# Experts over gathered tiles of 256 rows, in place of eight experts for every token

## The reference, cut to what matters

```python
x = x + 0.5 * ffn(layernorm(x))          # 8 experts, the best 2 of each token
x = x + attention(layernorm(x))          # 16 heads of 8 channels
x = x + 0.5 * ffn(layernorm(x))          # the same expert weights again

def ffn(x):                              # N = 4096 tokens
    logits = flat @ Wr.T                 # (N, 8)
    weights, ids = top_k(logits, 2)
    weights = softmax(weights)
    h = einsum('nc,efc->nef', flat, W1)  # 512 hidden columns: 256 values, 256 gates
    act = h[..., :256] * silu(h[..., 256:])
    y = einsum('nef,ecf->nec', act, W2)  # 256 -> 128
    return einsum('nec,ne->nc', y, router_weights)   # zero for 6 of the 8 experts
```

## Time and profile before

| | us |
|---|---|
| median of 3 runs (1358.19 to 1359.80) | 1358.84 |
| the profiled execution, whole | 1362.02 |
| its span, first to last instruction | 1360.2 |
| first expert stage and start: to the first product of attention | 356.2 |
| attention, from there to the last copy of its output | 703 |
| second expert stage | 301 |

### The profile page before, as it was taken

The page is one execution under the profiler, slowest core; times in us unless marked ns, Lnnn a source line. Parts: engine busy times, 40 slices in busy tenths (PEclk is TensorE's granted clock), DMA queues, the critical chain, the costliest instruction groups (busy, mean ns, idle before and its releaser), DMA issues.

```text
span 1360.2 us, 32042 instructions
## 1 busy us (share of the span) xinstructions
PE 1269.9 (93%) x10240; PEld 615.2 (45%) x10240; DVE 1112.3 (82%) x2306; ACT 816.2 (60%) x1540; POOL 142.5 (10%) x450
## 2 busy tenths in 40 slices
PE   5999999999899989999998999899989999999998
PEld 3766666666422222222222222222222677767776
DVE  7887877787779888888888888888886677777775
ACT  4433333333158888888888888888888423323332
POOL 1021112210211111111111111111110000000000
PEclk9999999999759999999999999999999999999999
DMA  6010111101221110101001100110011100000000
GB/s 201 1 47 14 36 47 47 47 21 28 67 60 31 31 39 30 29 29 39 30 29 33 36 30 29 37 32 29 29 41 31 40 26 26 26 22 13 24 3 15
DMA packets 52265, 48.49 MB, mean 36 GB/s; under 512 B 10080, under 2 KB 44768, under 8 KB 52192
## 3 DMA queue, kind: packets, MB, share of 16 engines
q1 hardware_dynamic: 52192, 47.61, 12.0%
HBM read 23.86 MB, written 23.33 MB: 35 GB/s over the span
## 4 chain that ended last, share of the span: by engine, by line
PE 82%; ACT 6%; issue 6%; DVE 4%; SPq 1%; ACTq 0%; DMA 0%; DVEq 0%
PE ps L765 22%; PE ps L906 19%; PE ps L893 18%; PE ps L752 15%; ACT probs L661 5%; PE ps L722 2%; PE ps L864 1%; DVE X L1092 1%; PE ps L742 1%; PE ps L686 1%; PE ps L883 1%; PE ps L729 1%; DVE act L1080 1%; PE ps L759 1%; SPq L320 0%
## 5 line engine op out<-in xcount | busy, mean ns | idle before, releaser
L1235 DVE TENSOR_REDUCE mx<-ps 128x1 f32<-128x1024 f32 x512 | 591.9, 1217 | 75.1 <-PE ps L864 69.4
L661 ACT ACTIVATE probs<-ps 128x512 f32<-128x512 f32 x1024 | 568.5, 594 | 93.0 <-PE ps L893 74.0
L906 PE MATMUL ps<-probs,vh 128*32 128x256 f32 x4096 | 329.6, 393 | 56.0 <-ACT probs L661 42.0
L590 ACT ACTIVATE sg<-ps,unscale 128x512 f32<-128x512 f32 x256 | 173.7, 687 | 307.0 <-PE ps L765 285.3
L893 PE MATMUL ps<-Q,K 51*128 51x512 bf16 x1024 | 333.2, 386 | 0.5 <-ACT probs L661 0.2
L864 PE MATMUL ps<-K,Q 48*128 48x512 bf16 x1008 | 328.1, 390 | 2.5 <-DVE mx L1235 2.0
L752 PEld LDWEIGHTS ps<-w,act 128*128 128x128 f32 x2048 | 247.9, 192 | 17.1
L752 PE MATMUL ps<-w,act 128*128 128x128 f32 x2048 | 249.0, 275 | 0.0
L1080 DVE SCALAR_TENSOR_TENSOR act<-ps,unscale,sg 128x512 f32<-128x512 f32 x256 | 183.5, 745 | 58.2 <-PE ps L765 19.8
L765 PE MATMUL ps<-x_hi,w_hi 128*128 128x512 f16 x512 | 194.6, 380 | 10.9 <-DVE act L1080 6.3
L1092 DVE SCALAR_TENSOR_TENSOR X<-ps,rw,X 128x128 f32<-128x128 f32 (+1 forms) x512 | 144.0, 344 | 61.9 <-PE ps L752 61.4
(11 more groups left out here) (84 smaller groups left out, 611.5 us busy)
## 6 DMA issues: line engine op xcount, KB each, us to landing
o_parts<-ot SPq DMA_DIRECT2D x64, 128.0 KB, 1.8
q_stack<-parts SPq DMA_DIRECT2D x48, 128.0 KB, 2.3
k_stack<-parts SPq DMA_DIRECT2D x48, 128.0 KB, 2.3
Q<-q_stack SPq DMA_DIRECT2D x64, 96.0 KB, 2.3
K<-k_stack SPq DMA_DIRECT2D x64, 96.0 KB, 2.3
probs<-w_in SPq DMA_DIRECT2D x8, 256.0 KB, 3.9
att<-o_parts SPq DMA_DIRECT2D x16, 128.0 KB, 2.6
rden<-rdens SPq DMA_DIRECT2D x16, 128.0 KB, 2.5
```

The source lines that it names most:

```text
L590: nc.scalar.activation(sg[:, j, :], hid[2 * j], ACT.Silu, scale=unscale[:, e, 2 + j:3 + j]).then_inc(silu_done, 1)
L661: nc.scalar.activation(probs[:, kb % PSLOTS, j * CH:(j + 1) * CH], score[i], ACT.Exp, scale=SCALE).then_inc(probs_ready, 1)
L906: last = nc.tensor.matmul(opsum[VW * c:VW * (c + 1), :], vh[:, u % 2, kb, :], probs[:, kb % PSLOTS, c * QW:(c + 1) * QW], start=(kb == 0), ...
L1235: nc.vector.tensor_reduce(mx[:, u % 2, t:t + 1], pair.rearrange("p a b -> p (a b)"), AX_X, ALU.max).then_inc(max_read, 1)
```

## The change

An expert stage is made of three steps that follow each other, where before one loop did everything.

1. **Gather** (`gather`, on all engines). For each of 4 batches of 1024 tokens: layernorm scaled by 2^11, router, two best experts. From membership matrices PE computes with small bf16 products (`places`) the place of each token within the region of its expert; a region has room for all tokens. POOL then sends the rows by indirect transfers (`scatter`): 16 for a batch, each 128 rows of 520 bytes (f16 high and low part, the number of the output row, the weight). DVE makes a table of 39 tiles from the counts (`make_table`): expert and first row of each. SP fills the ends of the regions with idle rows (`fill_pads`). 8192 rows need at most 39 tiles of 256, and always 39 are run.
2. **Tiles** (`experts`, written out 39 times). SP loads 256 rows into one of six slots (`load_tile`), PE transposes them, ACT copies them out of PSUM, and the products, silu and multiplication follow with half the former width. The expert comes from the table into a register (`value_load`) on PE, ACT and DVE, the first row into one on SP. DVE multiplies the output by the weight (`weigh`), and POOL sends it by two indirect transfers of 128 rows of 512 bytes to `y_rows` in HBM (`scatter_y`), where a token's two outputs lie side by side. A row slot is free again when the tile's output has landed.
3. **Add** (`add_y`). For each chunk of 512 tokens SP loads the pairs of rows (512 KB), and DVE adds both to X.

After the first stage the layernorm, projections, split and storing for attention now come chunk by chunk behind `add_y`, with no expert between. After attention, the output projection of three batches stands in the last head, that of the fourth in the gather. `store_out` follows `add_y` chunk by chunk. Attention itself is as it was. The diff, cut to its core:

```diff
+TILE = 256
+TH = TILE // P
+PICKS = 2
+TILES = PICKS * N // TILE + E - 1
+R_SLOTS = 6
+Y_SLOTS = 4
...
+            def load_tile(p, i):
+                g = TILES * p + i
+                back = g - R_SLOTS
+                if back >= 0:
+                    sp.wait_ge(y_stored[back % Y_SLOTS], 16 * TH * (back // Y_SLOTS + 1))
+                at = sp.value_load(row_at[0:1, i:i + 1], min_val=0, max_val=X_ROWS - TILE)
+                sp.dma_start(rows[:, g % R_SLOTS, :, :],
+                             x_rows[bass.ds(at, TILE), :].rearrange("(h p) w -> p h w", p=P)).then_inc(rows_loaded[g % R_SLOTS], 16)
+            def load_tiles(p):
+                fill_pads(p)
+                for s in range(2):
+                    sp.wait_ge(scattered[s], 16 * KB * PICKS * (2 * p + 2))
+                sp.wait_ge(padded, 16 * E * (p + 1))
+                for i in range(TILES):
+                    load_tile(p, i)
+                stored_tiles(sp, TILES * (p + 1))
...
+            def scatter(p, b):
...
+                pool.wait_ge(slots_ready, a + 1)
+                for t in range(KB):
+                    for k in range(PICKS):
+                        nc.gpsimd.indirect_dma_start(x_rows, bass.IndirectOffsetOnAxis(ap=slots[:, s, k, t:t + 1], axis=0),
+                                                     pay[:, s, t, k, :], None).then_inc(scattered[s], 16)
+            def scatter_y(p, i):
+                g = TILES * p + i
+                pool.wait_ge(y_ready, g + 1)
+                for h in range(TH):
+                    nc.gpsimd.indirect_dma_start(y_rows, bass.IndirectOffsetOnAxis(ap=rows[:, g % R_SLOTS, h, ID:ID + 1], axis=0),
+                                                 y_out[:, g % Y_SLOTS, h, :], None).then_inc(y_stored[g % Y_SLOTS], 16)
...
+            def rowsT_copy(p, i):
...
+                nc.scalar.activation(xrT[:, g % 2, :, :], rowsT, ACT.Copy).then_inc(xrT_ready, 1)
...
+                for i in range(TILES):
+                    silu(p, i)
+                    if i + 1 < TILES:
+                        rowsT_copy(p, i + 1)
...
+                for i in range(TILES):
+                    e = pe.value_load(expert_at[0:1, i:i + 1], min_val=0, max_val=E - 1)
+                    gates_of(p, i, e)
+                    if i + 1 < TILES:
+                        row_transposes(p, i + 1)
+                    vals_of(p, i, e)
+                    if before is not None:
+                        expert_out(p, i - 1, before)
+                    before = e
...
+            experts(0)
...
+            add_y(0, 0)
+            norm2(0)
+            for c in range(NCH - 1):
+                add_y(0, c + 1)
+                norm2(c + 1)
+                rotate(c, 0)
+                rotate(c, 1)
+                keep_values(c)
+                add_bias(c)
```

More of the change, by code:

```diff
@@ L58 @@
 VW = 32
-PIECE = H * CH // P
 QSLOTS = 4
@@ L611, in ffn @@
-            def ffn(p0, with_qkv):
-                def chunk(c, u, more=True, back=True, weights=False):
-                    ffn_chunk(p0 + c, u, more, c - 1 if back and with_qkv else None, weights)
-                chunk(0, 0, back=False, weights=with_qkv)
-                chunk(1, 1)
-                with sc.Fori(1, NCH // CPB - 1) as r:
-                    for u in range(CPB):
-                        chunk(CPB * r + u, u)
-                chunk(NCH - 2, 0)
-                chunk(NCH - 1, 1, more=False)
@@ L703, in w_transposes, with gather @@
                 for k in range(BLK):
-                    last = nc.tensor.transpose(wpsum[min(e, 1)][:, k * P:(k + 1) * P], w1_scaled[:, e % 2, k, :], ident[:])
+                    last = nc.tensor.transpose(wpsum[e % 4][:, k * P:(k + 1) * P], w1_scaled[:, e % 2, k, :], ident[:])
                 last.then_inc(wT_in_psum, 1)
+            def gather(p, weights, between=None):
+                for b in range(B):
+                    x_transposes(p, b, 0)
+                    x_transposes(p, b, 1)
+                    router(p, b)
+                    places(p, b)
+                    if weights:
+                        w_transposes(2 * b)
+                        w_transposes(2 * b + 1)
+                    if between and b == 1:
+                        out_projection(B - 1)
+                count_all(p)
@@ new lines, in experts @@
+            def experts(p):
+                pe.wait_ge(table_ready, p + 1)
+                before = None
+                row_transposes(p, 0)
+                for i in range(TILES):
+                    e = pe.value_load(expert_at[0:1, i:i + 1], min_val=0, max_val=E - 1)
[6 more added lines that the diff above has]
+                    before = e
+                expert_out(p, TILES - 1, before)
@@ L917, in _, with head @@
             pe.wait_ge(v_ready, NCH)
-            def head(r, u, maxes=True, row=True, first=False, early=None):
+            def head(r, u, maxes=True, row=True, first=False, early=False):
                 for i in range(HALVES):
@@ L982, in inverse_std @@
[L982 to L990 removed]
+            norms, routes = Order(dve, norm_order), Order(dve, route_order)
```

1156 lines of the change are left out of this document (635 added, 521 removed).

## The result

The recorded executions gave 1440.03 us as a median (1433.08 to 1441.74, four runs) for 1358.56 us of the kernel before: 1.0588 times the time, 95% interval 1.0552 to 1.0625. So the change made the kernel slower there, where I had forecast 1318 us.

What follows compares the result with a forecast made beforehand. PE was taken to bound both expert stages; from a 1360.2 us span, the first stage saves 7 us, the second 34, attention unchanged: 1319, or 1318 as a median. Range 1245 to 1440, likeliest case 1265 to 1356.

Runs made afterwards that it cites:

- both traces: Two profiles of the changed kernel, no edit between them: the recorded execution, span 1438.97 us, and a later run on another chip, median 1329.72 us.
- in time: The changed kernel, unedited, run again on another chip, where semaphore signals came at most 0.17 us behind their work: 1329.72 us, 0.9769 times the kernel before.

## What to carry to other kernels

When work moves to indirect transfers from POOL, count three prices: POOL's own time (1.26 us for 128 rows here), what POOL's other instructions and DVE's do to each other, and, on some chips, signals of PE and DVE that arrive only when a row of such transfers has ended. Measure such a kernel on more than one chip before judging it; the kernel before was the same everywhere, and that said nothing of the new one. And in a stage that is made of a chain through five engines, add up the waits of the chain and not the busy time of each engine.

## What the runs showed that I had not expected

- Semaphore updates of PE and DVE held for up to 3 to 4 us while POOL issues indirect transfers, most of them released 0.9 to 1.3 us after the end of one; seen on three of the six chips of the experiments, and in the recorded trace. Not in the tiles with plain transfers from POOL of the same size (0.54 us each), nor with SP's. In the same stretches a part of the signals has no record, and SP's own steps were slow.
- A reciprocal of 768 columns takes DVE 4.945 us and one of 256 columns 1.733, so 6.3 ns for each further column, where an addition of 512 columns takes 0.69 us alone, so 1.35 ns a column. The Trainium skill ("VectorE: DVE Perf Modes", section "First, the fixed hardware budget") says that it is an iterative divide; that a column of it costs more than four times a column of an addition is what these rows add.
- PE's granted clock is 0.50 in the second gather, the lower level (1.2 GHz), in both traces; PE had been busy 4.47 of the 11.8 us before it and is busy 20.32 of the 83.00 us in it. In the tiles that follow it is 0.94 on the mean, in time. POOL's row of transfers has no gap in that gather in time, so the clock cost nothing there.
